# Attention's opening in another order, and tile 1's low parts ahead of later tiles' passes

## The reference

```
h = layernorm(x)
s1 = (h @ W[:256]) @ a_w ;  s2 = (h @ W[256:]) @ a_w
e = s1[:, None] + s2[None, :] + a_b
e = where(e >= 0, e, 0.2 * e) ;  e = where(adj > 0, e, -9e15)
x = x + softmax(e, axis=1) @ (h @ fc_w + fc_b)
```

## Time and profile before

| | us |
|---|---|
| median of three runs (lowest, highest) | 1130.38 (1127.13, 1130.47) |
| the profiled execution's own time | 1126.45 |
| its span in the trace | 1124.7 |
| first turn of tile 0 on TensorE, start | 67.43 |
| TensorE, VectorE, ScalarE, GpSimd busy over the whole span | 1002.2, 846.6, 683.4, 356.7 |

### The profile page before, as it was taken

How to read it: one execution, slowest core, us unless ns; L and a number is a source line. 1 busy time by engine, 2 the same in 40 slices (tenths; PEclk the granted TensorE clock), 3 DMA queues, 4 the chain that set the end, 5 groups by cost and what they waited for, 6 DMA issues and landing times. The chain is left out here.

```text
span 1124.7 us, 23829 instructions
## 1 busy us (share of the span) xinstructions
PE 1002.2 (89%) x7842; PEld 802.4 (71%) x7842; DVE 846.6 (75%) x1942; ACT 683.4 (61%) x1083; POOL 356.7 (32%) x337
## 2 busy tenths in 40 slices
PE   5639999999999799989987999999299999999991
PEld 4529999989999789778753888888156666666661
DVE  5589999999995456876667466666468888888880
ACT  2769899888996277567652122221157777777771
POOL 0232323232232000008431044444214444444443
PEclk9859999999999789999999999999599999999995
DMA  9999999999953312220060999997713333333322
GB/s 375 240 315 296 287 286 285 284 289 284 290 173 93 117 38 76 76 76 39 1 122 1 230 213 280 253 259 208 262 35 58 58 57 59 57 59 54 57 40 24
DMA packets 76783, 177.27 MB, mean 158 GB/s; under 512 B 7952, under 2 KB 58000, under 8 KB 71440
## 3 DMA queue, kind: packets, MB, share of 16 engines
q1 hardware_dynamic: 54880, 121.45, 35.1%
q0 software_dynamic: 18128, 40.17, 20.0%
q10 hardware_dynamic: 3680, 14.42, 3.4%
HBM read 148.48 MB, written 49.68 MB: 176 GB/s over the span
## 5 line engine op out<-in xcount | busy, mean ns | idle before, releaser
L617 PE MATMUL PS<-G,PT 128*128 128x256 f16 x2028 | 233.7, 273 | 0.0
L617 PEld LDWEIGHTS PS<-G,PT 128*128 128x128 f16 x2028 | 198.5, 98 | 22.2
L1640 PE MATMUL PS<-W,X 128*128 x708 | 164.5, 382 | 4.8 <-issue 2.6
L1640 PEld LDWEIGHTS PS<-W,X 128*128 128x128 f16 x708 | 69.3, 98 | 84.6 <-issue 19.5
L1566 PE MATMUL PS<-own_H,adj_room 128*128 128x256 f16 x572 | 129.3, 273 | 0.0
L1564 PE MATMUL PS<-own_H,adj_room 128*128 128x257 f16 x572 | 129.3, 273 | 0.0
L1907 POOL DMA_INDIRECT out_dram<-X,place_i x59 | 92.2, 1563 | 99.0 <-DMA out_dram<-X,place_i 91.9
L601 PE MATMUL PS<-ident,probs 128*128 128x128 f32 x676 | 91.1, 281 | 24.5 <-ACT probs L349 16.4
L446 DVE SCALAR_TENSOR_TENSOR score<-S2low,S1low,S2row 128x3327 f32<-128x3327 f32 x25 | 105.7, 4230 | 0.0
L601 PEld LDWEIGHTS PS<-ident,probs 128*128 128x128 f32 x676 | 78.2, 145 | 30.2 <-issue 18.1
L464 DVE CUSTOM_DVE_ANT_0 score<-score,maskbias 128x3327 f32<-128x3327 f32 x25 | 90.6, 3625 | 7.7 <-DVE score L446 5.1
(11 more groups left out here) (283 smaller groups left out, 2060.8 us busy)
## 6 DMA issues: line engine op xcount, KB each, us to landing
adjf<-adj_dram SPq DMA_DIRECT2D x26, 1664.0 KB, 8.2
slot_rows<-blank SPq DMA_DIRECT2D x26, 1032.0 KB, 11.8
adj_room<-adjT_dram POOLq DMA_DIRECT2D x22, 832.0 KB, 10.6
block_of<-ew_dram SPq DMA_DIRECT2D x29, 512.0 KB, 5.5
adj_room<-ew_dram ACTq DMA_DIRECT2D x8, 1024.0 KB, 10.0
X<-slot_rows SPq DMA_DIRECT2D x59, 129.0 KB, 2.0
W<-ew_dram SPq DMA_DIRECT2D x9, 512.0 KB, 4.3
W_parts<-W SPq DMA_DIRECT2D x8, 512.0 KB, 2.9
```

Of the source, the lines that this page charges most:

```text
L617: mm = nc.tensor.matmul(acc[u][:, 0:D], left, right, start=(j == 0 and n == 0), stop=(j == T - 1 and n == 2))
L1640: mm = nc.tensor.matmul(psHE[u][:, n * F1:(n + 1) * F1], left[u][:, k, :], W1[:, e, k, part, n * F1:(n + 1) * F1], start=(m == 0), stop=(m ...
```

## The change

**ScalarE.** The opening runs `no_edge(0, 0)` and `spent` after the last `row_back`. `no_edge(2, 0)` moves from ahead of iteration 0 into it. Iteration 0 becomes hi(0,0), hi(0,1), hi(0,2), exponent(1), hi(0,3), no_edge(2), square_block(0), no_edge(3).

**VectorE.** The first masked part of tile 0 moves behind the second leaky part. `shift` of tiles 0 and 1 is done here and no more on GpSimd. `leaky(2)` goes into iteration 0, and the wait for the `fc_b` additions to the head of iteration 2. Iteration 0 becomes lo(0,0), reciprocal, lo(0,1), row scale, leaky(2), lo(0,3), masked(2). Iteration 1 becomes lo(1,0), reciprocal, leaky(3), lo(1,1), row scale, lo(1,3), masked(3), leaky(4). From iteration 2 on it is as before.

**GpSimd.** No shifts of tiles 0 and 1; in iteration 0 split(0) runs ahead of shift(2). Iteration 1 still has shift(3) ahead of split(1).

**TensorE.** Iteration 0: the four turns of tile 0, then its products 0 and 1. Iteration 1: turns 0 and 1 of tile 1, products(0,2), turn(1,2), products(0,3), turn(1,3).

```diff
 @block.gpsimd
             def iteration(t, u):
+                if isinstance(t, int) and t == 0:
+                    split(t, u, 2)
                 if live(t + 2):
                     shift(t + 2, u)
-                if live(t):
+                if live(t) and not (isinstance(t, int) and t == 0):
                     split(t, u, 2)
-            shift(0, 0)
-            shift(1, 1)
 @block.scalar
             def iteration(t, u):
+                first = isinstance(t, int) and t == 0
                 if live(t):
                     hi(t, u, 0)
+                if first:
+                    hi(t, u, 1)
+                    hi(t, u, 2)
                 if live(t + 1):
                     exponent(t + 1, 1 - u)
-                if live(t):
+                if live(t) and not first:
                     hi(t, u, 1)
                     hi(t, u, 2)
+                if first:
+                    hi(t, u, 3)
+                    no_edge(2, 0)
                 for n, at in enumerate(blocks_at(t)):
                     if n == 0:
                         square_block(t, n, at)
-                if live(t):
+                if live(t) and not first:
                     hi(t, u, 3)
...
-                else:
-                    nc.scalar.activation(spent[:, :], big[:, :], ACT.Exp, scale=-1.0).then_inc(exp_waits, 1)
-                    no_edge(0, 0)
...
             row_back(len(CK) - 1)
+            no_edge(0, 0)
+            nc.scalar.activation(spent[:, :], big[:, :], ACT.Exp, scale=-1.0).then_inc(exp_waits, 1)
             no_edge(1, 1)
             exponent(0, 0)
-            no_edge(2, 0)
 @block.vector
+            def shift(t, u):
+                dve.wait_ge(masked_ready, t + 1)
+                v.tensor_scalar(shift_by[u][:, :], rowmax[u][:, :], -1.0, LOG_P_SCALE, ALU.mult,
+                                ALU.add).then_inc(shift_ready, 1)
             def iteration(t, u):
-                if live(t + 2):
+                first = isinstance(t, int) and t == 0
+                if isinstance(t, int) and t == 2:
+                    dve.wait_ge(fcb_added, 16 * len(XG))
+                second = isinstance(t, int) and t == 1
+                if live(t + 2) and not first and not second:
                     masked(t + 2, u)
...
                     lo(t, u, 0)
                     invert_total(t, u)
+                    if second:
+                        leaky(t + 2, u)
                     lo(t, u, 1)
                     row_scale(t, u)
                 if live(t - 3):
                     row_stats(t - 3)
+                if first:
+                    leaky(t + 2, u)
                 if live(t):
                     lo(t, u, 3)
-                if live(t + 3):
+                if first or second:
+                    masked(t + 2, u)
+                if live(t + 3) and not first:
                     leaky(t + 3, 1 - u)
...
                         leaky_part(0, 0, early)
-                        masked_part(0, 0, early)
...
             leaky_part(1, early, N)
+            masked_part(0, 0, early)
             masked_part(1, early, N)
...
+            shift(0, 0)
             leaky(1, 1)
             masked(1, 1)
-            leaky(2, 0)
-            dve.wait_ge(fcb_added, 16 * len(XG))
+            shift(1, 1)
 @block.tensor
             def iteration(t, u):
+                if isinstance(t, int) and t == 0:
+                    for g in range(NG):
+                        turn(t, u, g)
+                    products(t, u, 0)
+                    products(t, u, 1)
+                    return
                 if live(t):
                     turn(t, u, 0)
                     turn(t, u, 1)
+                if isinstance(t, int) and t == 1:
+                    products(t - 1, 1 - u, 2)
+                    turn(t, u, 2)
+                    products(t - 1, 1 - u, 3)
+                    turn(t, u, 3)
+                    return
```

## The result

| | before | after |
|---|---|---|
| median of the runs taken side by side, us (14 of each) | 1128.41 (1125.98 to 1131.61) | 1133.41 (1130.25 to 1137.51) |
| ratio to before, with its 95% interval | | 1.004 (1.0029 to 1.0052) |
| the profiled execution: own time, span | 1126.45, 1124.7 | 1131.69, 1129.9 |
| start of masked(5) | 107.81 | 109.94 |

The changed kernel is slower by 4.5 us (the ratio) to 5.0 us (the medians). I had said +3.7 us and 1134.1.

What follows compares the result with a forecast made beforehand. TensorE and VectorE are full from about 90 us, so only pipeline entry counts: 8.4 us won at exponent(0), 1.6 left after the load wait, then +3.8 at masked(5), say +3.7, giving 1134.1; range 1127 to 1138.5.

Steps and rivals of the forecast that it cites:

- Part 1: The opening: last project no longer waits, shifts on VectorE; exponent(0) starts at 55.75 instead of 64.13, 8.4 us earlier.
- Part 2: Iteration 0: exponent(1) from 64.4, no_edge(2) done at 70.9, leaky(2) held by GpSimd's subtraction until 71.4.
- Part 3: ScalarE waits 6 us for square_block(0)'s load, landing unchanged at 76.9; of 8.4 us lead 1.6 are left.
- Part 4: Iterations 1 and 2: lead gone at masked(4), GpSimd shut out; masked(5) at 111.6 against 107.81, +3.8 us.
- the exclusion: At masked(4), masked and split(1)'s conversion and subtraction run one after another, from 96.7 to 103.6.
- rival 1: At masked(4), masked and GpSimd overlap freely: split(1) done at 100.0, sum +1.1 us, 1131.5; chance 0.25.
- masked doesn't exclude GpSimd: At masked(4), split(1) runs beside masked and is done at 100.0; +1.1 us, 1131.5; chance 0.25.
- The transfer lands early: square_block(0)'s load lands before 76.9, at 71 at best: -2.2 us, or -4.9 if masked and GpSimd overlap; chance 0.20.
- The later issue is lost: Tile 2's later adjacency issue delays square_block(0)'s load to 83: +9.8 us, 1140; chance 0.10.
- the forecast's three fifths of 0.45: Share of the main forecast's 0.45 chance counted as measurably slower, 0.28, with 1.5 us either way in the landing.
- rival 3: 6 us of tile 2's later adjacency issue are lost, square_block(0)'s load lands at 83: +9.8 us, 1140; chance 0.10.

Runs made afterwards that it cites:

- block 0 early: Changed kernel with the first load of block_of issued in the opening, right behind b1c, not behind tile 3's adjacency and blank rows; 1134.26 us, ratio 1.0037.
- blank rows late: Changed kernel with the blank rows of tiles 0 to 3 written at the end, not in the opening; 1128.16 us, ratio 1.0025.
- split(1) first: Changed kernel with GpSimd's split(1) ahead of shift(3) in iteration 1, nothing else; 1134.98 us, ratio 1.0039.
- no_edge(2) back and the relief: Changed kernel with blank rows of tiles 0 to 3 written at the end and no_edge(2) between exponent(0) and hi(0,0) again; 1122.22 us, ratio 0.9975.
- the old iterations and the relief: Changed kernel's opening, iterations as before the change, blank rows of tiles 0 to 3 written behind the last tiles; 1119.41 us, ratio 0.9940.
- the queue relieved: Blank rows of tiles 0 to 3 written behind the last tiles: new opening with iterations as before 1119.41 us (0.9940), changed kernel 1128.16 us (1.0025).
- the old iterations: Changed kernel's opening with all iterations ordered as before the change, fc_b wait at iteration 2; 1124.14 us, ratio 0.9994.
- the relief alone: Only the blank rows of tiles 0 to 3 written at the end: kernel before 1123.88 us (0.9983), changed kernel 1128.16 us (1.0025).

## Why the prediction held, and where it did not

**Part 1, right.** The last project starts at 42.88 and takes 1.91; exponent(0) starts at 55.09 against 55.75 forecast.

**Part 2, right but for who is held.** exponent(1) runs at 64.34, no_edge(2) from 67.65 to 70.73 (70.9 forecast). I had leaky(2) waiting for GpSimd's subtraction. It began first, at 64.84, and the subtraction was the one shut out (5.20 for 2.13); leaky(2) itself took 4.29; split(0)'s conversion, 64.61 to 65.65, lay over its first 0.8 us. Which of two instructions is held hangs on a few tenths of a microsecond, and here it made no difference, as nobody waited for split(0).

**Part 3, right.** This is the step that takes most of the lead away. 6 us of wait forecast and 5.38 seen, the square at 76.9 and at 76.12, hi(1,0) ending at 82.2 and at 81.12, VectorE's wait 6.5 and 6.54. The argument was that the sum of the bytes ahead of the load is the same, so that its landing is too. It held although the first transfer of the row, tile 2's adjacency, is issued 5.4 us later (50.73 against 45.37). In the two other executions the first square starts at 75.78 and 76.83. What the argument left out is the next load; I had priced only block 0. In the kernel as changed that hardly matters: tile 4's adjacency is issued at 70.91, and was at 70.42 before, and the second square is waited for by 0, 1.69 and 0.53 us in the three executions. The runs with block 0 early, and with the blank rows late, show that a larger second wait (5.95 and 4.17 us) stands right behind the first one.

**Part 4, right, and this is where the loss arises.** GpSimd's shift takes 3.46 us at 91.62 (3.5 near 93), exponent(3) waits for it (3.91 us), masked(4) and the subtraction exclude each other, raw is written at 101.74 (103.7), masked(5) starts at 109.94, 111.25 and 111.14 (111.6). The forecast had masked(4) 0.6 us late and masked(5) 3.8; the means are 0.4 and 3.4. So 3.1 us come between the two, of 3.2 forecast. I wrote that 2.7 us hang on the exclusion, the difference between the forecast's +3.8 and rival 1's +1.1 (2.3 in what I expected of split(1) first). With the meeting at masked(4) gone, that stretch took 12.06 us and not 14.64, 2.6 less. That bears the price out, in one execution, though the meeting only moved to masked(3) and the end didn't come earlier. How the kernel would do with no meeting at all, no run shows.

I took TensorE's waits as free. After the change TensorE waits six times for lo between 60 and 130 us, 17.0 us in all (15.3 and 16.9 in the other executions); before it was twice, 8.1 us; with no_edge(2) back and the relief five times, 11.4 us; with the old iterations and the relief twice, 8.5 us. The views of the waits, of the changed kernel and of the last:

```profile
PE PS L621 <- DVE PT L475: 17.0, 6, 6.7
```

```profile
PE PS L610 <- DVE PT L471: 8.5, 2, 7.5
```

(Columns: us in total, times, longest.) These are TensorE's waits for VectorE's lo; they are not a sum of losses, since an earlier start also counts as a longer wait. Behind masked(5) they cost the kernel as changed nothing, as residual(25) follows by the same 270.0 us. In two of the runs the lower clock cost TensorE 1.0 and 1.7 us there, a term that my sum doesn't have.

**The rivals.** *masked doesn't exclude GpSimd* is wrong: 4.35 for 3.62 and 5.28 for 2.13 in one meeting, 5.32 for masked in the other. The Trainium skill's rule ("SBUF — State Buffer", section "Who interferes with whom") holds in both directions. *The transfer lands early* is wrong for the kernel as changed (75.78 to 76.83 in three executions), and when the wait at that load was taken away (block 0 early, square at 70.90) nothing was won, where this rival, with the exclusion, gave 2.2 us below before. *The later issue is lost* is wrong for block 0.

**The sum.** Forecast +3.7; attention's part is +3.4 as the mean of three executions on each side, the whole +4.5 to +5.0. The remaining 1 to 2 us stay open. That the median of 1133.41 lies only 0.7 us from the forecast's 1134.1 is in part luck, for it was counted from three runs with a median of 1130.38, and the runs taken side by side had 1128.41. In the chances, slower by the forecast's three fifths of 0.45 (0.27) and rival 3's 0.10 is 0.37, not 0.40. The stretch behind attention, whose code is the same, took 746.9, 749.6 and 745.3 us in the three executions of before and 750.0, 755.2 and 746.0 after the change; the scatter is larger than the difference. In the pair of profiles that I compared, 3.5 us of it lie between 680 and 800 us; the window from 690 on, first of before, then of after:

```profile
690.00:700.00 10.00, 9.32 (x88) 8.09 (x87) 8.46 (x35) 0.88 (x2) 5.36 (x5) 1.00 1.03 294
```

```profile
690.00:700.00 10.00, 8.68 (x68) 7.12 (x67) 6.03 (x20) 3.20 (x4) 6.56 (x5) 0.88 1.00 233
```

TensorE does 20 matmuls fewer there, at a granted clock of 0.88. Whether an entry a few microseconds later causes that, no run here tells.

**What the change lost, then.** The opening is good for attention by 2.5 us as it is and by 6.1 us with the queue relieved (377.4 - 371.24). The new order of iterations 0 and 1 loses more than that: 5.9 us in the kernel as changed (380.7 - 374.83), 10.2 us with the queue relieved (381.41 - 371.24). The two are not made up alike. With the queue relieved the larger part, 4.9 us at masked(5), is no_edge(2) behind the four hi, which holds the next adjacency's issue while the DMA engines stand idle, 3.7 us are the order on the engines, and 1.7 us the lower clock in one execution. With the blank rows in place the DMA engines are never idle from 56 to 96 us (0.89 to 1.18 in every 2 us), ScalarE and SyncE stand from 76 us on where they stand with the old iterations, and the 5.1 us at masked(5) can't be no_edge(2)'s hold on a load. (VectorE waits 1.48 us for its bias ahead of masked(2), but stands 6.54 us behind it.) They are the passes in another order, and GpSimd shut out beside them, 2.6 us by the run with split(1) first. The rest was not taken apart between the engines. no_edge(2) back in its place alone, with the blank rows in place, was not tried.

## What to carry to other kernels

An instruction that frees a buffer is also the issue of the next load: before it is moved back behind other work, follow the queue of loads behind it, past the first one that is late. A wait for a saturated queue doesn't go away by taking one transfer to the front; take bytes out of the stretch, and make sure at the same time that the next issue isn't held by something else (here the relief alone gave under 2 us on either kernel and so did the new opening alone, both together 6 to 7). A part of a loss that is found in an altered kernel (here no_edge(2)'s, with the blank rows late) need not be a part of it in the kernel as it was: lay the two traces side by side and see where they come apart. Where an engine must wait for a load anyway, let the others have work in their queues that doesn't need what stands behind that wait.

## What the runs showed of the hardware

- In a saturated stretch the time of issue says little of the landing. Tile 2's adjacency was issued at 50.73 and not at 45.37, and block_of(0), the fourth transfer behind it on the queue, let its square start 0.85 us earlier than before. SyncE stood 7.20 us in the issue of that load (8.85 before), and was free of it at 65.79 and at 66.00.
- VectorE's leaky and its custom masked operation, each with two SBUF rows as inputs, and GpSimd's tensor operations shut each other out, and the later one is held for nearly the whole of the earlier: GpSimd's one-column shift took 3.46 us beside a leaky of 3.68, its subtraction 5.28 us beside a masked, and masked 5.32 us when it started 0.30 us into a subtraction.
- Such a meeting is easily moved and not so easily removed. With split(1) first masked(4) kept its 3.62 us and masked(3) took 5.32 in its stead; masked(5) came 0.8 us earlier and the end of attention no earlier.
- TensorE's granted clock fell in some executions for a few microseconds after it had stood idle: 30 products took 5.10 us at 0.58 and 0.57 (blank rows late) and 4.83 us at 0.55 to 0.60 (split(1) first), against 3.44 at 1.00 in the changed kernel, whose TensorE had stood idle for 2.15 us ahead of them too. What decides between the two, these runs don't show.
